# The bound for m summed in two halves of x behind the first weights, and constant scales for the first four sub-tiles

## The reference

```python
def reference(x, log_dt, B, inv_A_real, A_imag, attn_w, attn_b, ffn_W, ffn_b, A, Bm, Wr):
    # x (32 c, 128 h, 64 n, 2); h_ is (32, 128, 1024)
    dtA = (-exp(inv_A_real) + 1j * A_imag) * exp(log_dt)[:, None]
    Cc  = (B * x as complex numbers) * (exp(dtA) - 1) / A_complex
    h_  = 2 * einsum('chn,hnl->chl', Cc, exp(dtA[:, :, None] * arange(1024))).real
    h_  = h_ + layernorm(h_) @ attn_w.T + attn_b
    z   = layernorm(h_)
    gates = softmax(z @ Wr.T)
    return h_ + z @ ffn_W.T + ffn_b + sum_e 2 * gates[e] * ((z @ A[e].T) @ Bm[e].T)
```

## Time and profile before

| | us |
|---|---|
| median of 3 runs | 809.03 (808.96 to 809.17) |
| profiled execution, its own time | 807.61 |
| its span | 805.8 |
| PE busy | 769.3 (95%) |
| DVE busy | 622.0 (77%) |
| ACT busy | 527.3 (65%) |
| PE first busy above 90% without a break | from about 99 on |

### The profile page before, as it was taken

The page is one execution under the profiler, slowest core; times in us unless marked ns, Lnnn a source line. Parts: engine busy times, 40 slices in busy tenths (PEclk is TensorE's granted clock), DMA queues, the critical chain, the costliest instruction groups (busy, mean ns, idle before and its releaser), DMA issues.

```text
span 805.8 us, 14896 instructions
## 1 busy us (share of the span) xinstructions
PE 769.3 (95%) x5334; PEld 377.3 (47%) x5334; DVE 622.0 (77%) x1229; ACT 527.3 (65%) x881; POOL 5.5 (1%) x22
## 2 busy tenths in 40 slices
PE   2759899999999999999999999999999999999997
PEld 1634344444444444444444444444444444444443
DVE  7899978777777787787878877777887778777532
ACT  6778876667676766766677576667766676765210
POOL 2000000000000000000000000000000000000000
PEclk9988999999999999999999999999999999999999
DMA  7869942434343333334333342434324333433323
GB/s 287 295 123 173 153 81 55 98 67 86 80 95 62 70 80 78 78 75 99 80 67 71 67 98 55 99 80 83 70 57 95 70 83 80 93 61 71 57 53 81
DMA packets 196109, 74.65 MB, mean 93 GB/s; under 512 B 184496, under 2 KB 189488, under 8 KB 195960
## 3 DMA queue, kind: packets, MB, share of 16 engines
q1 hardware_dynamic: 195992, 74.26, 42.8%
q10 hardware_dynamic: 96, 0.13, 0.0%
HBM read 14.06 MB, written 16.78 MB: 38 GB/s over the span
## 4 chain that ended last, share of the span: by engine, by line
PE 86%; DVE 4%; SPq 4%; ACT 2%; DMA 2%; issue 1%; ACTq 0%
PE ps_g L531 39%; PE ps_g L591 37%; PE ps_a L522 5%; PE ps_g L597 2%; PE ps_g L697 1%; PE ps_p L579 1%; SPq L378 1%; SPq L361 1%; DMA x<-in_L_attn_weight 1%; DVE wa_lo L1238 1%; DMA x<-x_tok 1%; PE ps_p L581 1%; ACT phase L736 0%; SPq L437 0%; DMA x<-stage 0%
## 5 line engine op out<-in xcount | busy, mean ns | idle before, releaser
L531 PE MATMUL ps_g<-wa_hi,x 128*128 128x512 f16 x1024 | 271.6, 381 | 8.3 <-DMA wa_lo<-h_tok 7.2
L591 PE MATMUL ps_g<-wf_hi,x 128*128 128x512 f16 x992 | 261.0, 379 | 0.2 <-DMA wf_lo<-stage 0.2
L531 PEld LDWEIGHTS ps_g<-wa_hi,x 128*128 128x128 f16 x1024 | 98.0, 98 | 130.6 <-issue 16.2
L531 PE MATMUL ps_g<-wa_lo,x 128*128 128x512 f16 x512 | 154.5, 381 | 0.0
L591 PE MATMUL ps_g<-wf_lo,x 128*128 128x512 f16 x496 | 148.8, 379 | 0.0
L591 PEld LDWEIGHTS ps_g<-wf_hi,x 128*128 128x128 f16 x992 | 94.9, 98 | 110.7 <-DMA wf_lo<-stage 0.7
L1198 DVE SCALAR_TENSOR_TENSOR result<-ps_g,unscale,h_tok 128x1024 f32<-128x1024 f32 x31 | 39.8, 1284 | 88.2 <-PE ps_g L597 88.2
L768 ACT ACTIVATE junk<-ps_a,stat 128x1024 bf16<-128x1024 f32 x32 | 35.2, 1101 | 68.8 <-DVE stat L1105 68.8
L531 PEld LDWEIGHTS ps_g<-wa_lo,x 128*128 128x128 f16 x512 | 50.2, 98 | 60.6 <-issue 0.8
L591 PEld LDWEIGHTS ps_g<-wf_lo,x 128*128 128x128 f16 x496 | 48.5, 98 | 58.3
L774 ACT ACTIVATE junk<-h_tok,stat 128x1024 bf16<-128x1024 f32 x32 | 36.8, 1149 | 52.2 <-DVE stat L1145 52.2
(11 more groups left out here) (214 smaller groups left out, 881.4 us busy)
## 6 DMA issues: line engine op xcount, KB each, us to landing
out<-result SPq DMA_DIRECT2D x124, 128.0 KB, 2.2
stage<-in_L_ffn_W SPq DMA_DIRECT2D x8, 512.0 KB, 14.1
x_raw<-in_x SPq DMA_DIRECT2D x38, 64.0 KB
wf_hi<-in_x SPq DMA_DIRECT2D x1, 2048.0 KB, 9.1
h_tok<-in_L_attn_weight SPq DMA_DIRECT2D x2, 512.0 KB, 4.1
x<-in_L_attn_weight SPq DMA_DIRECT2D x2, 512.0 KB, 8.1
result<-in_L_attn_weight SPq DMA_DIRECT2D x2, 512.0 KB, 9.5
x<-x_tok SPq DMA_TRANSPOSE x64, 3.2
```

The source lines that it names most:

```text
L531: mm = pe.matmul(ps[:, o, :], x1_part(part, ps is ps_g2)[:, k, :], ws[:, k, o * HALF:(o + 1) * HALF], start=k == 0 and part == 0 and ws is ...
L591: pe.matmul(ps_g2[:, o, :], xs[:, k, :], ws[:, k, o * HALF:(o + 1) * HALF], start=k == 0 and xs is x2_hi and ws is wf_hi, stop=False)
```

## The change

- The 2 MB copy of `x` and its one sum of squares are gone from the start. In their place `load_x_half(k)` loads 1 MB into the area of `u_split`, twice, and `square_x_half(k)` sums its squares (128x2048) on ACT. The first load stands on SP ahead of `turn_x1(0, 0)`; the second stands behind `load_x(1)`, waits for the first sum, and stands ahead of `turn_attn_weight(6)`. The sums stand on ACT behind `attn_hi(5)` and behind `high_1(0, 1)`.
- `copy_x(0)` stands ahead of `phases(0, 0)`, and `high_1(0, 0)` ahead of `attn_hi(2, 3)`.
- `q` is copied out of PSUM without a factor, so `m` of the first four sub-tiles carries none. These sub-tiles use constants and the new tiles `whole_eps` and `whole_bias` in place of `m_unscale`, `m_mean`, `m_bias` and `m_eps`.
- All of `scale_m`, now ten instructions, and `scale_q`, two that multiply `q1` and `q2` in place, stand on DVE between `make_m(1, 1)` and `make_u(1, 1)`. POOL's maximum over the partitions for it stands last there.
- `turn_lora(0, 0)` stands ahead of `turn_lora_b()`. On DVE the two steps of t = 1 are written out ahead of the loop.

```diff
             load_weight(0, 2)
-            sp.dma_start(x_all, x.rearrange(...)).then_inc(s_x_all, 16)
             load_x(0)
...
             sp.wait_ge(s_norm, 2)
+            load_x_half(0)
             turn_x1(0, 0)
             load_x(1)
+            load_x_half(1)
             turn_attn_weight(6)
...
             turn_weights(13, 16)
+            turn_lora(0, 0)
             turn_lora_b()
-            turn_lora(0, 0)
...
+            def load_x_half(k):
+                if k == 0:
+                    sp.wait_ge(s_pre_dve, PRE)
+                else:
+                    sp.wait_ge(s_x_squares, 1)
+                sp.dma_start(x_half, x.rearrange("c (b h) n r -> (c b) (h n r)", b=4)[:, 2 * L * k:2 * L * (k + 1)])\
+                    .then_inc(s_x_half[k], 16)
...
+            def square_x_half(k):
+                act.wait_ge(s_x_half[k], 16)
+                act.wait_ge(s_pre_dve, PRE)
+                at_least(act, s_x_squares, k)
+                act.activation(x_half_junk, x_half, ACT.Square, accum_out=m_top[:, k:k + 1]).then_inc(s_x_squares, 1)
...
-            act.wait_ge(s_m_scale, 4)
-            act.activation(q1..., ps_g1[:, 0, :], ACT.Copy, scale=m_mult)
+            act.activation(q1..., ps_g1[:, 0, :], ACT.Copy)
...
+            def scale_q():
+                dve.wait_ge(s_m_scale, 10)
+                for q in (q1, q2):
+                    dve.tensor_scalar(q[:, :, :], q[:, :, :], m_mult, None, ALU.mult).then_inc(s_q, 1)
+                dve.wait_ge(s_q, 4)
...
+                down, mean, added = (1 / USCALE, -USCALE / L, whole_bias[:, :]) if is_whole(T, i) else (m_unscale, m_mean, m_bias)
...
             make_m(1, 1)
+            scale_m()
+            scale_q()
             make_u(1, 1)
```

More of the change, by code:

```diff
@@ L93, in program @@
         eps = sb("eps", [P, 1])
+        whole_eps = sb("whole_eps", [P, 1])
+        whole_bias = sb("whole_bias", [P, 1])
         q1 = sb("q1", [P, KA, H])
@@ L328, in program, with is_whole @@
         lbb = params[:, KB * (ER + P // 2):KB * (ER + P // 2 + 1)]
+        def is_whole(T, i):
+            return isinstance(T, int) and 2 * T + i < WHOLE
         def after(t, i):
@@ L847, in _ @@
             act.activation(z_turn[:, :], ps_a[:, 0, 0:P], ACT.Copy).then_inc(s_pre_act, 1)
+            copy_x(0)
             act.wait_ge(s_pre_act, 6)
             phases(0, 0)
-            act.wait_ge(s_x_all, 16)
-            act.activation(x_all_junk, x_all, ACT.Square, accum_out=m_top[:, 0:1]).then_inc(s_x_squares, 1)
-            copy_x(0)
             act.wait_ge(s_bias, 16)
@@ L856, in _ @@
             act.wait_ge(s_pre_pe, 3)
-            act.wait_ge(s_m_scale, 4)
-            act.activation(q1[:, :, :].rearrange("p a b -> p (a b)"), ps_g1[:, 0, :], ACT.Copy, scale=m_mult)\
+            act.activation(q1[:, :, :].rearrange("p a b -> p (a b)"), ps_g1[:, 0, :], ACT.Copy)\
                 .then_inc(s_q, 1)
             act.wait_ge(s_pre_pe, 4)
-            act.activation(q2[:, :, :].rearrange("p a b -> p (a b)"), ps_a[:, 0, :], ACT.Copy, scale=m_mult)\
+            act.activation(q2[:, :, :].rearrange("p a b -> p (a b)"), ps_a[:, 0, :], ACT.Copy)\
                 .then_inc(s_q, 1)
@@ L869, in _ @@
             square_1(0, 0)
-            rstd_guess(0, 0, stat_1, s_ssq1, s_log1, s_y1, m_eps)
+            rstd_guess(0, 0, stat_1, s_ssq1, s_log1, s_y1, whole_eps[:, :])
+            high_1(0, 0)
             attn_hi(2, 3)
-            high_1(0, 0)
             decays(0, 1)
@@ L875, in _ @@
             sines(0, 1)
-            attn_hi(5, 6)
+            attn_hi(5)
+            square_x_half(0)
+            attn_hi(6)
             ffn_hi(8, 9)
@@ L1045, in low_u, with scale_m @@
                     .then_inc(s_u_lo, 1)
-            def scale_m(first, end):
+            def scale_m():
                 dve.wait_ge(s_m_top, 1)
[L1050 to L1071, removed]
@@ new lines, in scale_m @@
+                dve.tensor_scalar(m_power, m_top[:, 3:4], m_top[:, 4:5], m_top[:, 5:6], ALU.add, ALU.mult)\
+                    .then_inc(s_m_scale, 1)
+                dve.wait_ge(s_m_scale, 1)
+                dve.tensor_scalar(m_power, m_power, 1e-10, None, ALU.max).then_inc(s_m_scale, 1)
+                dve.wait_ge(s_m_scale, 2)
+                dve.tensor_scalar(m_power.bitcast(U32), m_power.bitcast(U32), 1, EXPONENT, ALU.logical_shift_right,
+                                  ALU.bitwise_and).then_inc(s_m_scale, 1)
@@ new lines, in scale_m @@
+                dve.wait_ge(s_m_scale, 3)
+                dve.reciprocal(m_mult, m_power).then_inc(s_m_scale, 1)
+                dve.tensor_scalar(m_unscale, m_power, ROOT / (WSCALE * USCALE), None, ALU.mult).then_inc(s_m_scale, 1)
+                dve.wait_ge(s_m_scale, 5)
+                dve.tensor_scalar(m_mult, m_mult, WSCALE / ROOT, None, ALU.mult).then_inc(s_m_scale, 1)
+                dve.wait_ge(s_m_scale, 6)
+                dve.tensor_scalar(m_whole, m_mult, USCALE, None, ALU.mult).then_inc(s_m_scale, 1)
@@ L1101, in keep_h @@
                 dve.wait_ge(s_s4, J + 1)
-                dve.scalar_tensor_tensor(out=h_tok[:, i, :], in0=whole(ps_a), scalar=m_unscale, in1=bias_bc[:, :],
+                down, mean, added = (1 / USCALE, -USCALE / L, whole_bias[:, :]) if is_whole(T, i) else (m_unscale, m_mean, m_bias)
+                dve.scalar_tensor_tensor(out=h_tok[:, i, :], in0=whole(ps_a), scalar=down, in1=bias_bc[:, :],
                                          op0=ALU.mult, op1=ALU.add, accum_out=stat_1[:, 0:1]).then_inc(s_htok, 1)
                 dve.wait_ge(s_htok, J + 1)
-                dve.tensor_scalar(stat_1[:, 1:2], stat_1[:, 0:1], m_mean, m_bias, ALU.mult, ALU.add)\
+                dve.tensor_scalar(stat_1[:, 1:2], stat_1[:, 0:1], mean, added, ALU.mult, ALU.add)\
                     .then_inc(s_nm1, 1)
@@ L1374, in _ @@
             assert done[0] == PRE
-            scale_m(0, 4)
             round_turns(0, 0)
@@ L1378, in _ @@
             make_m(0, 0)
-            scale_m(4, 6)
             dve.wait_ge(s_bias_act, 1)
@@ L1460, in step @@
                 low_2(t, i)
-            with dve.Fori(1, TILES - 1) as t:
+            step(1, 0, True)
+            step(1, 1, True)
+            with dve.Fori(2, TILES - 1) as t:
                 step(t, 0, True)
```

41 lines of the change are left out of this document (22 added, 19 removed).

## The result

The changed kernel takes 812.93 us (median of 7 runs, 811.34 to 814.84) against 808.94 (7 runs, 807.74 to 809.17) for the kernel before: ratio 1.0057, 95% interval 1.0045 to 1.0068. It is 4.0 us slower; 811.2 was predicted, in a range of 809.3 to 813.8. The profiled execution is the slowest of the seven: 814.84, span 813.0, against 807.61 before.

What follows compares the result with a forecast made beforehand. PE, busy 95%, bounds the kernel, so only the start of `attn(1, 0)` counts. `make_u(1, 1)` late by 0.80 + 2.7 = 3.5, with 1.3 in hand, gives 809.03 + 2.2 = 811.2 us; range 809.3 to 813.8.

Steps and rivals of the forecast that it cites:

- the first rival: The second 1 MB load delays the transposes behind it and PE's restart, or the clock falls: 812.7 or 813.1; chance 0.17.
- The front: At the start, without the 2 MB load and sum, `q` is turned at 20.15 instead of 21.41: 1.26 us gained.
- The order of `high_1(0, 0)`: ACT makes `high_1(0, 0)` before splitting block 2, so `turn_weight(4)` starts at 40.25 against 41.20: gain down to 0.95.
- The clock in `turn_weight(4)`: Its eight transposes take 1.04 or 1.90 us by PE's clock; the middle was taken, 0.45 gained, bounds 0 and 0.86.
- The first sum: The first half's sum takes 1.96 us on ACT, moving `attn_hi(6)` by +0.56 and DVE to +0.24.
- The second sum: Another 1.96 us on ACT ahead of `ffn_hi(10)`; with 1.40 in hand, 0.56 reaches DVE, then at +0.80.
- PE's restart: PE's start after its wait for the last attn part's transposes, 60.61 before, was to come later by under 1 us.
- `scale_m` and `scale_q`: Twelve DVE instructions between `make_m(1, 1)` and `make_u(1, 1)`: 1.8 and 0.9 us, together 2.7, bounds 1.5 and 3.3.
- 1.3 us in hand at `make_u(1, 1)`: `make_u(1, 1)` may come 1.3 us later before it sets the start of `attn(1, 0)`; beyond that each microsecond counts.
- The fall of the clock ahead of `s4(1, 1)`: In the longer PE gap ahead of `s4(1, 1)` the clock may fall, costing up to 1.93 us again: 813.1.
- (a): Term of the theory after the result: the scale on DVE costs 2.65 us, in full.
- (d): Term of the theory after the result: the clock at `s4(1, 1)`; no size given in that list.

Runs made afterwards that it cites:

- no_second_sum: The changed kernel with the second half of x still loaded but not summed on ACT, a constant in its place: 813.16 us, ratio 1.0063.
- no_second_load: The changed kernel without the load of the second half of x, the second sum running over the first half again: 811.75 us, ratio 1.0040.
- order_back: The changed kernel with `attn_hi(2, 3)` ahead of `high_1(0, 0)` on ACT again: 812.54 us, ratio 1.0052.
- late_scale: The changed kernel with `scale_m` and `scale_q` moved on DVE behind `low_2(0, 1)`: 810.35 us, ratio 1.0027.
- warm_s4: The changed kernel with 5 and 9 filler matmuls on PE ahead of and behind `turn_x(2)`: 811.93 us, ratio 1.0047.
- no_sums: The changed kernel with neither loads nor sums of the two halves, a constant standing for the bound: median 811.32 us, ratio 1.0023.
- one_early_sum: The changed kernel with the 2 MB load and one sum back at the start in place of the halves, and the late scale: 811.2 us, ratio 1.0032.

## Why the prediction was right, and where it was not

The number landed in the range, but not by the forecast's own case. That case had `attn(1, 0)` later by 1.2 to 3.2 us, and 0.57; the median moved by 4.0. What came was the first rival, the loads and the clock in the way, which had 0.17 and its own sums of 812.7 and 813.1. The direction and most terms were sound; that 812.93 lies inside is owed to a range drawn wide enough for that rival, and in part luck. Term by term:

- **Direction and bound: right.** Nothing happened behind `attn(1, 0)` but the first matmuls at half clock; the change was worth what it moved ahead of it.
- **The front, -1.26: right.** `q` was turned 1.44 earlier and y made 1.05 earlier.
- **The order of `high_1(0, 0)`, gain down to 0.95: a bit too good.** At the start of `turn_weight(4)` it was 0.70.
- **The clock in `turn_weight(4)`, -0.45: mis-sized.** It took 1.97 against 1.90. The lower bound was right: nothing gained. I chose the middle between two idle stretches of 2.5 and 5 us; the clock fell 2 to 3 us into this one. The reading given there in brackets, that the longer gap gains nothing, was the right one.
- **The first sum, +1.96: right in size** (1.91, with the accumulator's read). `attn_lo(6)` came to +0.97, where +0.24 was forecast; the 0.73 between them are the two terms above.
- **The second sum, +0.56 on DVE: a bit too large** (1.34 - 0.97 = 0.37 more), and it set nothing: no_second_sum took it away and gained nothing.
- **PE's restart "later by under 1": wrong.** It came 2.94 later. This is the step that failed: I let DVE carry the delay from 62 us on and gave "the loads get in the way of the transposes" 0.17. It happened in all five profiles in which load 1 stood right ahead of block 6's transposes, with issues of 3.06 to 3.19 in place of 1.23. Its price, by no_second_load, is 1.2 in the median, not clear of the spread. The rival as I wrote it was close: landing 5.4 after issue where I had up to 4.5, and about 1 us in hand at `keep_h2(0, 0)` (in order_back 2.99 late at the restart, 2.03 there). SP's row of transposes went with it, which late_scale shows: `attn(1, 0)` there waits for x1 until 100.99.
- **`scale_m` and `scale_q`, +2.7: right.** 2.65 in the profile. Moving them gave 2.6 in the median, with the clock ahead of `s4(1, 1)` in it.
- **1.3 us in hand at `make_u(1, 1)`: right.** At full clock `s4` would have ended at 103.4, 4.6 late, for a `make_u` 6.06 late.
- **The fall of the clock ahead of `s4(1, 1)`: named as part of the rival, up to 1.93 extra.** In the profiled run 1.71 in `s4` and 0.8 behind it. Over the executions it is worth about 1.0 by warm_s4, not clear of the spread.
- **The clock's return behind PE's restart: put at nothing without a reason.** It came near 69.4 in the changed kernel and 66.3 in order_back, and moved `keep_h2(0, 0)` by 1.5.

The forecast of 811.2 was 1.7 short of 812.93; no_second_load and warm_s4 account for 1.2 and 1.0 against it. What I can't settle is how these split in a typical execution: the differences of the medians are as large as the spread of a few runs, and they overlap, as late_scale removes (a) and much of (d) together. The Trainium skill's page "DMA: Bandwidth & Descriptors", section "Queues, rings and completion order", says that each DMA engine takes descriptors in ring order. The same sentence adds that a later descriptor may still finish its write first, so that the rule gives an order of starting and no size. These runs agree with it: the load landed at 55.9, the two transposes behind it at 57.0 and 58.0, which is 5.4 and 5.1 us after their issue, and 3.2 and 3.3 without the load. So it spoke for this rival, and was a reason to give it more than 0.17.

## What to carry to other kernels

Ask of a large load not only when its data is needed but what small, urgent DMA is issued right behind it on the same queue: here 1 MB made transposes right behind it land 2 us late at two places of the queue, and at a third, with no transpose right behind it, it delayed none. Work that is needed late is put behind the instruction that PE waits for, not ahead of it; moved behind the next two steps, `scale_m` was no longer what PE waited for. And a wait of 2 us on TensorE can cost two more in the clock behind it, so an idle stretch that a change makes or mends belongs in the sum with both prices, clock held and clock fallen.

## What the runs showed of the hardware

- **Half clock after short idle stretches, and not each time.** Ahead of `s4(1, 1)` PE was idle 2.13 (the changed kernel), 2.04 (no_sums), 2.07 (order_back), 2.32 (no_second_load), 2.07 (one_early_sum) and 1.84 (no_second_sum); the same 32 matmuls took 3.64, 3.64, 3.33, 3.19, 2.70 and 1.93 us. The length of the idle stretch does not tell them apart.
- **The return to full clock differs too.** The timeline and windows of the changed kernel have PE busy from 63.55 and at half clock until 69; in order_back it started at 63.60 and was at full clock by 67. The window of the changed kernel, then that of order_back:

```profile
69.00:70.00 1.00, 1.00 (x5) 0.45 (x4) 0.51 (x1) 1.00 (x3) 0.14 (x1) 0.81 0.94 179
...
66.00:67.00 1.00, 1.00 (x5) 0.45 (x4) 1.00 (x2) 0.60 (x1) 0.00 (x0) 0.86 0.98 181
```

That fits the 1.5 us between the times at which `keep_h2(0, 0)` could start (71.79 and 70.28), and would spread the runs of one kernel by itself.
- **SP's issue stalls, not only the transfer.** The first transpose behind the load was issued in 1.27, the second needed 3.06, and those behind it 1.34 again. The 1 MB load itself took 0.38 to issue. The first load, at 36.21 ahead of `turn_x1(0, 0)`, made the one transpose right behind it land 5.5 after issue as well; that cost nothing, since the other transpose of `turn_x1(0, 0)` was issued only at 41.60.
